# Moving three steps of the first attention from VectorE to ScalarE, and its output guard from five passes to four

## The reference, cut to what matters

```python
h = nan_to_num(layernorm(x), nan=0, posinf=1e4, neginf=-1e4)   # layernorm: (x - m) / sqrt(v + 1e-5)
Q, K, V = h @ wq.T, h @ wk.T, h @ wv.T        # 16 heads of 16
Q, K = rotate(Q), rotate(K)
probs = softmax(where(allowed_key, Q @ K.T / 4, lowest))      # 25 first and 128 last keys allowed
V[..., 129:, :] += gated V[..., 128, :]       # the gate: from the last row of probs
x = x + nan_to_num((probs @ V) @ wo.T, nan=0, posinf=1e4, neginf=-1e4)
```

## Time and profile before

| | us |
|---|---|
| time before, median of 3 executions | 943.53 (941.61 to 945.49) |
| the profiled execution's own time | 944.91 |
| its span, first to last instruction | 942.9 |
| PE busy | 856.5 (91%) |
| DVE busy | 717.7 (76%) |
| ACT busy | 531.3 (56%) |
| POOL busy | 434.7 (46%) |

### The profile page before, as it was taken

How to read it: one execution, slowest core, us unless ns; L and a number is a source line. 1 busy time by engine, 2 the same in 40 slices (tenths; PEclk the granted TensorE clock), 3 DMA queues, 4 the chain that set the end, 5 groups by cost and what they waited for, 6 DMA issues and landing times.

```text
span 942.9 us, 19230 instructions
## 1 busy us (share of the span) xinstructions
PE 856.5 (91%) x6286; PEld 649.1 (69%) x6286; DVE 717.7 (76%) x2366; ACT 531.3 (56%) x1392; POOL 434.7 (46%) x683
## 2 busy tenths in 40 slices
PE   6678898889999999987999999999999997999996
PEld 5556666667765666655888787887888775666663
DVE  6567988889778887663968787787868686888872
ACT  5356544454354555545676676757586761555555
POOL 0348898887766665446202121221202012556655
PEclk9779999999999999989999999999999999999999
DMA  6333333332223557102112020202021022234331
GB/s 211 60 50 49 53 56 55 56 55 38 35 37 58 103 118 133 43 14 46 24 24 46 1 46 1 45 2 46 2 45 37 11 35 35 36 71 59 59 48 35
DMA packets 49938, 46.55 MB, mean 49 GB/s; under 512 B 5280, under 2 KB 47280, under 8 KB 49840
## 3 DMA queue, kind: packets, MB, share of 16 engines
q1 hardware_dynamic: 49840, 45.33, 26.2%
HBM read 11.40 MB, written 2.10 MB: 14 GB/s over the span
## 4 chain that ended last, share of the span: by engine, by line
PE 33%; DVE 15%; issue 3%; ACT 1%; POOL 1%; DMA 0%; POOLq 0%; SPq 0%; DVEq 0%; ACTq 0%
PE bank L301 8%; PE bank L1979 6%; PE bank L1987 4%; PE bank L1913 4%; DVE weights L1476 3%; PE bank L1928 3%; DVE weights L1466 3%; PE bank L1743 2%; PE bank L1756 2%; DVE q_lo L1456 1%; PE bank L1739 1%; DVE rope L1454 1%; PE bank L1782 1%; DVE xn L338 1%; DVE arena L1313 1%
## 5 line engine op out<-in xcount | busy, mean ns | idle before, releaser
L1313 DVE TENSOR_REDUCE arena<-bank 128x2 f32<-128x512 f32 (+1 forms) x192 | 130.9, 685 | 42.4 <-PE bank L1743 41.4
L924 ACT ACTIVATE weights<-bank 128x512 f32<-128x512 f32 x144 | 85.8, 596 | 109.1 <-PE bank L1756 108.3
L1006 ACT ACTIVATE weights<-weights,neg_max 128x128 f32<-128x128 f32 (+1 forms) x256 | 113.9, 449 | 39.2 <-DVE neg_max L1466 38.7
L727 POOL TENSOR_SCALAR_AFFINE_SELECT weights<-weights 128x256 f32<-128x256 f32 x144 | 68.6, 478 | 101.4 <-ACT weights L924 101.4
L1979 PE MATMUL bank<-kbT,arena 128*128 128x128 f32 (+1 forms) x512 | 105.1, 328 | 1.0 <-DVE y L447 0.9
L667 POOL TENSOR_SCALAR weights<-weights 128x512 f32<-128x512 f32 x64 | 97.6, 1537 | 12.5 <-ACT weights L832 12.5
L1743 PE MATMUL bank<-kf_stack,q_stack 96*128 96x256 f32 (+1 forms) x256 | 99.7, 432 | 0.0
L1013 ACT ACTIVATE weights<-bank 128x384 f32<-128x384 f32 x128 | 62.7, 490 | 61.0 <-PE bank L1987 60.5
L1466 DVE CUSTOM_DVE_ANT_0 weights<-bank,arena 128x128 f32<-128x128 f32 (+1 forms) x256 | 80.2, 350 | 14.6 <-PE bank L1979 12.6
L301 PE MATMUL bank<-x_hi,wb_hi 128*128 128x256 f32 x256 | 83.8, 327 | 2.8 <-DVE q_lo L1456 2.8
L1476 DVE TENSOR_SCALAR weights<-weights,inv_sum 128x128 f32<-128x128 f32 (+1 forms) x256 | 81.3, 360 | 4.6
(11 more groups left out here) (236 smaller groups left out, 2514.2 us busy)
## 6 DMA issues: line engine op xcount, KB each, us to landing
q_stack<-q_hi SPq DMA_DIRECT2D x96, 128.0 KB, 4.5
arena<-arena SPq DMA_DIRECT2D x64, 128.0 KB, 2.5
q_stack<-q_lo SPq DMA_DIRECT2D x48, 128.0 KB, 5.3
ka_stack<-k_hi SPq DMA_DIRECT2D x32, 76.5 KB, 2.8
x_all<-x SPq DMA_DIRECT2D x8, 256.0 KB, 5.1
st_wo<-b_wo SPq DMA_DIRECT2D x8, 256.0 KB, 4.2
arena<-b_wqn SPq DMA_DIRECT2D x8, 256.0 KB, 3.3
out<-x_all SPq DMA_DIRECT2D x8, 256.0 KB, 2.1
```

Of the source, the lines that this page charges most:

```text
L924: a.activation(s["pT"][(STEPS * b + k) % N_PT], p2[k % 2][:, :], ACT.Exp).then_inc(s["exp"], 1)
L1006: last = a.activation(p, p, ACT.Exp, scale=-1.0, bias=neg_max[:, h % 4, t:t + 1], accum_out=sums[:, h % 4, t:t + 1])
L1313: v.tensor_reduce(into, p1[k % 2][:, :].rearrange("p (s g k) -> p s g k", s=n, g=NC), AX.X, ALU.max, negate=True).then_inc(s["maxed"], 1)
```

## The change

From the third batch on (iterations 0 to 5) `xn` is made by ACT at k=9, after its copies of the values, as `rstd * x + x_shift`; POOL makes `neg_mean` and `x_shift = -mean * rstd` for it, right after `rstd` and ahead of the rotation. The copy of 64 columns behind `hT` and the repetition of `x_lo` go from DVE to ACT. The output guard is now: clamp from the bank, NaN to a number by a minimum and maximum from the bank (at k=13), mask from the bank (k=14), and a copy from the bank under the mask (k=15); PE's next write of that bank waits for all four.

```diff
             g.tensor_tensor(rstd[:, :], var_eps[:, :], expo[:, :], ALU.pow).then_inc(s["rstd"], 1)
+            if s is sa:
+                g.tensor_scalar(neg_mean[:, :], mv[:, :, 0], -1.0, None, ALU.mult).then_inc(sa["shift"], 1)
+                g.wait_ge(*at(s, "rstd", b, 2))
+                g.wait_ge(*at(sa, "shift", b, 1))
+                g.tensor_tensor(x_shift[:, :], neg_mean[:, :], rstd[:, :], ALU.mult).then_inc(sa["shift"], 1)
...
-                    residual(sa, b - 3, guard_t, at(sa, "guarded", b - 3, 5))
+                    residual(sa, b - 3, guard_t, at(sa, "guarded", b - 3, 4))
...
+                if k == 3 and there(b + 1):
+                    act.wait_ge(*at(sa, "x_lo", b + 1, 1))
+                    a.activation(rep_lo[:, :, :].rearrange("p c (g k) -> p c g k", g=G),
+                                 x_lo[:, :, 0:VC].bitcast(f32).unsqueeze(2).to_broadcast([P, NC, G, VC]),
+                                 ACT.Copy).then_inc(sa["rep"], 1)
...
+                if k == 9 and b >= 0 and there(b + 2):
+                    act.wait_ge(*at(sa, "shift", b + 2, 2))
+                    act.wait_ge(*at(sa, "xT", b + 2, 0))
+                    for t in range(NT):
+                        last = a.activation(xn[:, t, :], x_tile(b + 2, t), ACT.Identity, scale=rstd[:, t:t + 1],
+                                            bias=x_shift[:, t:t + 1])
+                    last.then_inc(sa["xn"], 1)
...
                 if k == 13 and there(b + 2):
+                    act.wait_ge(*at(sa, "hT", b + 2, 2))
+                    act.wait_ge(*at(sa, "x_lo", b + 2, 0))
+                    a.activation(hT[:, :, T:TX], hT[:, :, 0:TX - T], ACT.Copy).then_inc(sa["hT"], 1)
                     act.wait_ge(*at(sa, "hT", b + 2, 3))
...
-                link(sa, "guarded", b, 1, v.tensor_scalar(guard_t, ps_r[:, :], 0.0, None, ALU.max))
-                v.scalar_tensor_tensor(guard_z, ps_r[:, :], 0.0, guard_t, op0=ALU.min, op1=ALU.add)\
+                link(sa, "guarded", b, 1, v.tensor_scalar(guard_z, ps_r[:, :], -BIG, BIG, ALU.max, ALU.min))
+                v.scalar_tensor_tensor(guard_t, ps_r[:, :], 0.0, guard_z, op0=ALU.min, op1=ALU.max)\
...
                 if i == 0:
-                    ins = v.tensor_scalar(m, guard_z, 0.0, 0.0, ALU.mult, ALU.is_equal)
-                elif i == 1:
-                    ins = v.tensor_scalar(guard_t, guard_z, -BIG, BIG, ALU.max, ALU.min)
+                    ins = v.tensor_scalar(m, ps_r[:, :], 0.0, 0.0, ALU.mult, ALU.is_equal)
                 else:
-                    ins = v.copy_predicated(guard_t, m, guard_z)
+                    ins = v.copy_predicated(guard_t, m, ps_r[:, :])
...
-                if k == 3 and there(b + 1):
-                    repeat_lo(b + 1)
...
-                if k == 6 and there(b - 3):
-                    guard_inf(b - 3, 2)
...
-                if k == 9 and there(b + 2):
+                if k == 9 and b < 0 and there(b + 2):
                     dve_normalize(sa, b + 2)
...
+                if k == (13 if b <= B else 15) and there(b - 2):
+                    guard_nan(b - 2)
                 if k == (14 if b <= B else 15) and there(b - 2):
-                    guard_nan(b - 2)
-                if k == 15 and there(b - 2):
                     guard_inf(b - 2, 0)
...
-                    wait_since(pe, sa, "guarded", b - 1, 2)
+                    wait_since(pe, sa, "guarded", b - 1, 4)
...
-                    pe.wait_ge(*(at(sa, "guarded", B - 1, 2) if s is sf[0] and (b, o) == (0, 0) else at(s, "y", b, 3 * o)))
+                    pe.wait_ge(*(at(sa, "guarded", B - 1, 4) if s is sf[0] and (b, o) == (0, 0) else at(s, "y", b, 3 * o)))
```

More of the change, by code:

```diff
@@ L93, in hybrid_layers_kernel @@
         rstd = sb("rstd", [P, NT])
+        x_shift = sb("x_shift", [P, NT])
+        neg_mean = sb("neg_mean", [P, NT])
         xn = sb("xn", [P, NT, D])
@@ L155, in hybrid_layers_kernel @@
                      e_dve=11, e_exp=3, v_ps=1, v_big=1, v_small=1, b_ps=1, v_done=1, rep=2, s_ps=H, maxed=H,
-                     clamped=2, sT_ps=2 * ITEMS, exp=2 * ITEMS, guard=8, guard_first=2, yT_ps=1, yT=1, wo_ps=NT, guarded=5)
+                     clamped=2, sT_ps=2 * ITEMS, exp=2 * ITEMS, guard=8, guard_first=2, yT_ps=1, yT=1, wo_ps=NT, guarded=4,
+                     shift=2)
         sf = [signals("ffn", "f", **TURNED, q_ps=1, kg_ps=2, k_sel=3, k48=3, kT_ps=1, k_stack=1, v_ps=1, v_sel=2,
@@ L312, in dve_stats @@
             if s is sa:
+                wait_since(v, sa, "shift", b, 0)
                 v.wait_ge(*((s_x, 16 * (B - 1)) if b else (s_x0, 16)))
             else:
+                if s is sf[0] and b == 0:
+                    v.wait_ge(*at(sa, "shift", B - 1, 2))
                 v.wait_ge(*at({"f": sa, "b": sf[0], "g": sm}["g" if s is sf[1] else s["kind"]], "x_done", b, 1))
@@ L327, in pool_rstd @@
             g.wait_ge(*at(s, "rstd", b, 1))
+            if s is sa:
+                wait_since(g, sa, "xn", b, 0)
+            elif s is sf[0] and b == 0:
+                g.wait_ge(*at(sa, "xn", B - 1, 1))
             g.tensor_tensor(rstd[:, :], var_eps[:, :], expo[:, :], ALU.pow).then_inc(s["rstd"], 1)
+            if s is sa:
+                g.tensor_scalar(neg_mean[:, :], mv[:, :, 0], -1.0, None, ALU.mult).then_inc(sa["shift"], 1)
+                g.wait_ge(*at(s, "rstd", b, 2))
+                g.wait_ge(*at(sa, "shift", b, 1))
+                g.tensor_tensor(x_shift[:, :], neg_mean[:, :], rstd[:, :], ALU.mult).then_inc(sa["shift"], 1)
         def dve_normalize(s, b):
@@ L904, in step_a @@
                 if k == 13 and there(b + 2):
+                    act.wait_ge(*at(sa, "hT", b + 2, 2))
+                    act.wait_ge(*at(sa, "x_lo", b + 2, 0))
+                    a.activation(hT[:, :, T:TX], hT[:, :, 0:TX - T], ACT.Copy).then_inc(sa["hT"], 1)
                     act.wait_ge(*at(sa, "hT", b + 2, 3))
-                    act.wait_ge(*at(sa, "x_lo", b + 2, 0))
                     act.wait_ge(*at(sa, "tok_ps", b + 2, 0))
@@ L1180, in turn_x @@
                 link(sa, "hT", b, 1, v.tensor_scalar(h_pos[:, :, :], halves(ps_a), 0.0, BIG, ALU.max, ALU.min))
[L1181 to L1191, removed]
+                v.scalar_tensor_tensor(hT[:, :, 0:T], halves(ps_a), 0.0, h_pos[:, :, :], op0=ALU.min, op1=ALU.add)\
+                    .then_inc(sa["hT"], 1)
             def last_row_least(b):
```

## The result

The changed kernel takes 955.52 us (median of 4 executions, 951.73 to 956.1) against 942.85 (941.61 to 945.49) for the kernel before, run on the same chip: a ratio of 1.0125 (1.0105 to 1.0145), that is 11.8 us slower; the two medians lie 12.7 apart. All ratios leave out two disturbed executions, one of 4258 us in e1 and one of 2005.7 us of the kernel before in the round of e14 to e17. The forecast was 946.0, its range 937 to 952; the time is outside it, on the slow side. The nearest case was rival A, the clock, with 952.

The account below looks back on a forecast made before the run. It took a loop through DVE, ACT, POOL, ACT and PE, about 27 us an iteration, as the bound. Terms of 0.5 + 0.9 + 0.75 + 3 x 0.2 - 0.8 + 0.5 = +2.45 us gave 946.0, range 937 to 952.

Parts of the forecast that it names:

- rival A: PE's wait before the transposes becomes one long stretch; clock halves in two more iterations, four falls, +6 us: 952; chance 0.24.
- PE's wait of 1.17 goes: PE's 1.17 us wait for DVE before the scores of k=5 disappears; counted as evidence against more clock falls.
- the loop: Chain setting the iteration's period: DVE 10.9, ACT 2.3, POOL 6.15, ACT 2.2, PE 5.6 us, about 27.
- On the loop it is worth nothing: Moving xn off DVE frees 2.57 us there but gains nothing, covered by POOL's rotation and ACT's work after it.
- ACT's `xn`: Two tiles between ACT's copies and PE's transposes: +0.9 us an iteration, bounds 0.7 and 1.2.
- POOL's two: Two small instructions ahead of POOL's rotation: +0.5 us an iteration together, bounds 0.4 and 0.7.
- The guard's passes: Mask 0.68 and copy 0.75 us replace 1.28 with 1.43 on DVE: +0.15, bounds -0.1 and +0.5.
- DVE's stretch: DVE's work from L1196 to the rotation of the queries shrinks 0.95 us; PE lets all of it through.
- The last batch: PE turns two passes (1.4 us) later, but what follows waited for DVE in any case: +0.5 us.
- Iterations 6 to 9: No xn and one DVE pass less: -0.2 us each from PE's few waits for DVE, -0.8 together.
- Rival B: DVE is the bound after all; PE's waits of 1.31 or 1.17 us come out: 936 to 938; chance 0.16.
- Rival C: The DVE-POOL port lock works more widely, freeing POOL of say 0.8 us an iteration: 943, no change; forecast with it 0.57.

Follow-up runs that it names:

- e1: The changed kernel with xn back on DVE and without POOL's two small instructions; guard and copies stay: 939.66 us, 0.9966 of before.
- e14: The kernel before plus POOL's two small instructions ahead of the rotation, with seven small matmuls in TensorE's waits in iterations 0 to 5: 943.67 us, 1.0012 of before.
- e17: The changed kernel with POOL's two small instructions behind the rotation of q instead of ahead: 950.29 us, 1.0077 of before.
- e4: The changed kernel with seven small matmuls in TensorE's two waits at k=11, iterations 0 to 5: 945.65 us, 1.0032 of before.
- e9: The kernel before plus only POOL's two small instructions ahead of the rotation, their results never read: 949.24 us, 1.0071 of before.
- e8: The kernel before with only the guard in four passes and its new order: 938.19 us, 0.9954 of before.
- e16: The kernel before with only the two copies (repetition of x_lo, copy behind hT) moved to ACT: 939.34 us, 0.9962 of before.
- e5: The kernel before with one small matmul more before the transposes at k=11, iterations 0 to 5: 941.43 us, 0.9982 of before.
- e15: The kernel before plus only POOL's two small instructions, put behind the rotation of q, their results never read: 942.63 us, 1.0001 of before.
- e11: The changed kernel with four small matmuls in TensorE's first wait at k=11 only, none before the transposes: 953.41 us, 1.0119 of before.

## Why the prediction was wrong

**The step that failed** is the term for the clock, which the sum put at nothing, and with it the weighing of rival A. The text named the mechanism: with DVE free, PE "does its scores at once and waits in one long stretch, about 3.3 us of idle instead of 2.1, before the transposes". That is what the timelines show (2.59 and 1.45 us). But the sum held the clock where it was, and A had a chance of 0.24 only, against which stood that "PE's wait of 1.17 goes". That wait lies at k=5, some 10 us ahead of the transposes, and did not go either: 0.68 us of it are left in iteration 5. What the runs showed in its place: the matmuls in TensorE's waits give back 5.6 us in e14 and 8.8 in e4, and by the estimate above 6 to 8 of the 11.8 us are clock. The other 4 to 6 us lie on the loop, where the sum had 2.45, so its terms were too small as well.

**A came nearest, and that is partly luck.** Its price was four more falls at 1.5 us, 6 us in all, and that is about the clock's share; the falls came in iterations 1 to 5 and lasted longer, 51.2 us at the low level against 27.3. But its 952 stands on the sum's 946, which was too low for the loop.

**"On the loop it is worth nothing" was half of the truth on `xn` leaving DVE.** It gained nothing. But its 2.57 us had also set when PE did its last score, and with that how PE's idle time lay. The Trainium skill (SBUF — State Buffer, "SBUF: two separate sides") calls the port pair of VectorE and GpSimd an exclusive lock, and the prediction drew from it that DVE's time was mostly blocked time. The trace of e9 agrees, with 0.74 us for the same two tiles when the rotation has not begun. I had not asked what the freed engine's promptness does to PE.

**The other terms of the sum**, one by one. With all their misses put right the sum would come to some 8 us, more than the 4 to 6 of the loop, so not all of each lies on the loop; that split stays open.

- ACT's `xn`: taken at 0.9, measured 1.09 us for two. From the figures of the Trainium skill (ScalarE: Activation LUTs, "What ACT_TABLE_LOAD costs") the estimate had been 1.08, and the trace agrees with it. Six times 0.19 is 1.1 us.
- In iterations 0 and 1 the sum had no `xn` on ACT at all, and gave no reason. In iteration 0 the transposes, which before came without a wait, waited 3.19 us for it, and the difference grew by 2.1 us there, where the sum had 0.5:

```profile
51.42 1.09 PE L362 MATMUL bank<-cst,xn 128*128 128x128 f32 x4 [3.19 <-ACT xn L916]
```

- POOL's two: taken at 0.5, measured 1.36 - 0.79 = 0.57 there and 0.67 in the mean of six iterations. Their place costs 4.5 us by e17, against 6 x 0.5 = 3.0.
- The guard's passes: mask 0.68 and copy 0.75 taken, 0.68 and 0.73 measured (medians by source line below). `k_lo` without the copy beside it: -0.3 taken, and the slow one is gone (longest 0.88 us, before 1.15).
- DVE's stretch: from L1196 (L1214 after) to the end of DVE's part of the rotation of q, for iteration 5, it was 10.90 us and is 10.29: -0.61, where -0.95 was taken net of the guard's place. The sum let all of it through because it is under 1.17. It did not go through: PE still waits 0.68 there. e8, e16 and e1 fit that limit from the other side: parts worth 4.3 and 3.6 us alone give 3.2 together. (Some of the two gains can be clock: their low level is at 45 and 46 us, e1's at 52.)
- The last batch: the wait before the turning grew from 0.55 to 2.06 us (taken: 1.4 more), and the stretch around it, from transposes to transposes, from 303.7 - 280.8 = 22.9 to 316.1 - 292.7 = 23.4: +0.5, as taken.
- Iterations 6 to 9: -0.8 taken, and not there: the difference stands at 11.7 to 11.9 us through them.

Passes and `k_lo` in the changed kernel by source line (shortest/median/longest in ns), as the earlier trace rows:

```profile
L1150 DVE TENSOR_SCALAR arena<-bank x8: 676/676/694, 113.9 to 297.0; 128x512 int32<-128x512 f32 x8
```

```profile
L1152 DVE COPY_PREDICATED arena<-arena,bank x8: 719/730/743, 114.9 to 297.7; 128x512 f32<-128x512 int32 x8
```

```profile
L671 POOL TENSOR_TENSOR k_lo<-arena,k_hi x7: 858/872/876, 43.3 to 211.4; 128x320 fp32r<-128x320 f32 x7
```

```profile
298.57 0.63 PE L449 MATMUL bank<-cst,oT 128*128 128x128 f32 x4 [2.06 <-issue]
```

The last row is that of the timeline of PE for the last batch, as the earlier trace rows.

e4, the change with its waits filled, is at 1.0032, that is 945.9 on the median of before, and the forecast was 946.0. That nearness is luck: e4 has also lost the falls that the sum left standing (41 us at the low level against 53), and the loop's share was more than the sum's.

**Rival B** (DVE is the bound, 936 to 938) is out for `xn`, but holds in part for the small parts: of PE's wait of 1.17 us 0.78 and 0.68 are left, and e8 and e16 land near its border. **Rival C** (the lock works more widely) did not show: POOL's two passes of the rotation take 1.09 and 1.26 us after, 1.09 and 1.27 before, and only `k_lo` got shorter.

**What stays open**: what the kernel before would gain with its own three falls of the clock removed (e5 was too weak a try), and with it the exact share of the clock; which of PE's waits, or their sum, brings a fall; and how the loop's share divides among its terms. Of the expectations e1, e8, e14 and e16 came out faster than any range they gave, e9 slower, and e17 between its two ranges.

## What to carry to other kernels

Before an engine is relieved, follow what its lateness does to TensorE: here two tiny instructions ahead of a hand-over took its waits from 1.1 to 2.1 us an iteration to 2.0 to 3.8, and the clock, which had fallen around the transposes of three iterations, fell around those of five. Take the clock from all executions, not from the profiled one alone, and fill the waits of the kernel before too, as a control. Put small new instructions behind the hand-over that others wait for, not ahead of it (0.1 against 6.7 us here), and new work into an idle stretch of its engine rather than at its place in the old order. Run the parts of a change alone: here two gained 4.3 and 3.6 us, not in sum, and the third lost more than both.

## What was not expected of the hardware

- Two GpSimd instructions of 0.20 to 0.40 us on 128x2, which nothing reads, made the kernel 0.71% slower where they stood ahead of the rotation and 0.01% where they stood behind it (e9, e15).
- Two VectorE `tensor_scalar` of 128x256 take 0.74 us beside such small GpSimd instructions and 2.57 beside a GpSimd `tensor_tensor` of 128x512 (e9 against the earlier trace rows and e15).
- Seven matmuls an iteration (fourteen records), which compute nothing that is used, made the changed kernel 0.93% faster (e4), with the granted clock at 1.00 in windows where it had been 0.50; four of them in the first of two waits only brought 0.06% (e11).
